# A decoder layer on one core: another order of the eight attention units, and no filler matmuls between them

## The chip, the cores and the metric

One core of a Trainium2 chip runs the whole program; nothing is shared with other cores. The metric is the device time of one execution in microseconds. A core has engines with a queue of their own each: TensorE (PE: matmuls and transposes), VectorE (DVE), ScalarE (ACT), GpSimd (POOL), and SyncE (SP), which issues the loads and stores. An engine works through its queue in order; a step that waits for a semaphore holds up all that stands behind it.

## The reference

The layer works on x of 8 batches x 128 tokens x 256 features, in three stages, each added to its input and normalized:

```python
x = layernorm(x + attn(x, Wq, Wk, Wv, Wo))      # 16 heads of 128, 4 K/V groups, rotary, softmax
x = layernorm(x + xattn(ctx, ctx, x, ssm, D))   # per head of 8 features: y_ij = conv(k_i * v_j) + D k_i v_j
                                                # out_j = sum_i y_ij * q_i     (16 heads, length 256)
x = layernorm(x + ffn(x, W_gate, W_qkv))        # top-1 gated shared key/value, causal softmax, 16 heads
```

The second stage's convolution acts on the product of context features only, and doesn't depend on x; only the last sum (its "products") does.

## The kernel before, in words

**Phase A, attention.** The work is cut into 8 units. A unit is one K/V group (4 query heads, `HG`) for one half of the batches (4 batches, `BH`). They run in the order u = 2v + j, group v = 0..3 outside, half j = 0, 1 inside, so half 0 has all its groups after unit 6, half 1 after unit 7. Within a unit k = 0..3 is the batch. For each batch there are `scores` (TensorE), `row_max` (VectorE), `exps` (ScalarE), `invert` (VectorE), `normalize` (GpSimd), `turn` (TensorE transposes the probabilities), `prob_high` (ScalarE) and `prob_low` (VectorE), which split them into a high and a low part, `values` (three matmuls; the third takes the low part), `head_copy` (ScalarE), `head_low` (VectorE), `output` (12 matmuls with Wo into an accumulation bank); `accumulate` (VectorE) adds two batches' output to x.

**Between these steps** a unit does the projections for the next unit, its "items" K, Q0 to Q3 and V. For K and Q: `project` (6 matmuls) into one of two banks that take turns, `rotate` on ScalarE (two copies into `rot`), `cos_item` on VectorE (frees the bank), `sin_item` on GpSimd (L1574) and `add_item` on VectorE (L1126). So item i + 2 waits for the cos step of item i. `rot` and `t_cos`, `t_sin` have two buffers each. Each group's weights are loaded once (`w_raw`) and split into `w_hi` (ScalarE, L835) and `w_lo` (VectorE, L1138) in even units; Wo's are split by ScalarE (`wo_hi`) and GpSimd (`wo_lo`, L1599).

**Convolutions.** The items C0 to C3 of each unit are four of the 32 convolutions (L394) of the second stage, of one matmul call (even) or two (odd). GpSimd prepares the products of context features for four of them with `pairs` (L1564, eight instructions), in two buffers.

**Unit 7** has no next unit. Here the second stage begins for batches 0 to 3: `first_stats(0)`, GpSimd's `power` for the reciprocal root, `first_apply(b)`, `x1_turn(b)` (TensorE), `mix_query(b)` (ScalarE), the products (`pair_products`, L318 and L321, 15 instructions a batch, mostly on GpSimd; the nearest three distances of batch 0 on VectorE), `mix_sum(b)` (VectorE, L1376), `mix_turn(b)`, `add_mix(b)`, statistics, `second_power`, `second_apply(b)`, `x2_turn(b)`. These turns all use one bank, `mix_bank`. Where TensorE would wait, `keep_busy(n)` (L417) puts n filler matmuls: 26 in unit 7 and behind it.

**Phase B.** `seq(i)` for i = 0..6 runs the third stage of batch i, with parts of the next batches' second and third stage between: `gate_project`, `kv_project`, `query_project`, `key_turn`, `fscores`, `fexps`, `fturn`, `fvalues`, `y_turn` and the last normalization.

The order on each engine is written out by hand, and each wait is a count on a semaphore.

Of the kernel before, what the change touches and what calls it, by code (L numbers as in the profile page):

```python
# [21 lines left out]
P = 128  # L22
# [25 lines left out]

COLS = ["K", "Q0", "Q1", "Q2", "Q3", "V"]
FRONT = ["K", "Q0", "Q1", "Q2", "Q3", "V"]  # L50
BODY = ["K", "Q0", "Q1", "Q2", "Q3", "C1", "C2", "C3", "C0", "V"]
LAST = ["C1", "C2", "C3"]
# [3 lines left out]
def decoder_kernel(nc, xt_d, x_d, wqkv_d, wo_d, toep_d, dcoef_d, ctx_d, wf_d, cos_d, sin_d, ident_d,  # L56
                   anti_d, causal_d, ties_d, out_d):
    ctx = ExitStack()
    with ctx:
# [3 lines left out]
        def sem(name):  # L63
# [60 lines left out]
        prod = q_rope[:, :, :, :].rearrange("p n h t -> p n (h t)").rearrange(  # L124
            "p n (a j i) -> p n a j i", j=HD, i=HD)
# [3 lines left out]
        qmix = rot[:, :, 0:D]  # L129
# [30 lines left out]
        first_conv_bank = acc_bank[1]  # L160
        fscore_bank = [bank[4], bank[5], bank[3]]
# [62 lines left out]
        ln3 = [sem(f"ln3_{n}") for n in ("sum", "stats", "aggr", "eps", "rstd", "out")]  # L224
        x1T_done = sem("x1T_done")
# [100 lines left out]
        def _(sp):  # L326
            def load_toep(u, j):

                if not (isinstance(u, int) and u <= 1):
                    sp.wait_ge(proj_done, proj_count(u - 2, BODY.index("C3")))  # L330
                sp.dma_start(toep[:, j, :, :], toep_d[:, bass.ds(2 * u, 2), :]).then_inc(in_toep[j], 16)
# [9 lines left out]
            load_toep(0, 0)  # L341
# [24 lines left out]
        def _(pe):  # L366
# [32 lines left out]
            def scores(u, j, k):  # L399
# [20 lines left out]
            pe.wait_ge(filler_set, 1)  # L420
            keep_busy(13)
            pe.wait_ge(x_hi_done, 1)
            pe.wait_ge(w_hi_first, 1)
            for name in COLS:
                if name == "V":
                    pe.wait_ge(cos_done, 1)
                if name == "Q2":
                    pe.wait_ge(w_lo_done, 2)
                project(0, name, front_bank[name], first=(name == "K"))
            def front_scores(k, heads):  # L430

                for h in heads:
                    if k == 0:
# [1319 lines left out]
```

## Time and profile before

| | us |
|---|---|
| median of 3 runs | 339.44 |
| lowest and highest run | 336.38, 342.62 |
| profiled execution: span from the first to the last instruction | 334.2 |
| between that span and the lowest, median, highest run | 2.2, 5.2, 8.4 |
| TensorE busy in the span | 316.0 |
| VectorE, ScalarE, GpSimd busy in the span | 253.1, 232.3, 198.7 |

The profiled execution's time outside of its span isn't recorded, so the span stands for it. Busy times of TensorE are modelled: a row's duration reaches some 0.2 us beyond the start of the next matmul's, so that its steps are best read from start to start. In the span, unit 0 starts at 21.25 us, unit 1 at 49.83, unit 2 at 75.60, unit 3 at 101.36, unit 6 at 178.64 and unit 7 at 204.38; the first `fscores` is at 233.04 and that of the second batch at 246.54.

### The profile page before, as it was taken

The page shows a single profiled execution, that of the slowest core. Times are in us where ns is not written, and L with a number is a line of the kernel's source. Part 1 is how long each engine was busy: PE and PEld are TensorE (multiplying, and loading weights), DVE is VectorE, ACT ScalarE, POOL GpSimd, SP SyncE. Part 2 cuts the span into 40 slices and gives each one's busy share as a digit, 9 for nine tenths or more (in the row PEclk, how much of TensorE's full clock was granted, in tenths as well). Part 3 has the DMA queues.
Part 4 walks back from the last instruction along what each step waited for, and adds up shares of the span by engine and source line. Part 5 has one row for each costly group of instructions (what it writes and reads, how often), then busy time and mean ns, then how long its engine had stood idle before and what let it go on. Part 6 is the DMA issues. An engine that isn't in the chain of part 4 may idle for free.

```text
span 334.2 us, 6299 instructions
## 1 busy us (share of the span) xinstructions
PE 316.0 (95%) x2099; PEld 245.1 (73%) x2099; DVE 253.1 (76%) x505; ACT 232.3 (69%) x691; POOL 198.7 (59%) x284
## 2 busy tenths in 40 slices
PE   6998999999999999999999999999699999999982
PEld 2786798898898888888889888755366566666641
DVE  2698867857867856876865776989877899998646
ACT  3679578768868957968867865531458777878781
POOL 0679835837844857754665763799790866812102
PEclk9999999999999999999999999999979999999998
DMA  6941010042010031010040000000000000000010
GB/s 178 352 194 63 2 33 0 1 127 66 0 31 0 3 127 64 0 33 0 0 138 4 1 0 2 1 2 1 0 1 2 2 16 3 17 19 18 1 33 31
DMA packets 5616, 13.08 MB, mean 39 GB/s; under 512 B 848, under 2 KB 3024, under 8 KB 5328
## 3 DMA queue, kind: packets, MB, share of 16 engines
q1 hardware_dynamic: 5312, 12.29, 11.0%
q10 hardware_dynamic: 272, 0.39, 0.4%
q8 instruction: 17, 0.28, 0.3%
q14 instruction: 15, 0.12, 0.1%
HBM read 11.63 MB, written 1.05 MB: 38 GB/s over the span
## 4 chain that ended last, share of the span: by engine, by line
PE 77%; DVE 8%; POOL 6%; issue 3%; ACT 2%; DMA 2%; POOLq 0%; DVEq 0%
PE bank L377 19%; PE bank L532 11%; PE bank L408 8%; PE bank L394 6%; PE bank L704 4%; PE bank L693 4%; PE bank L497 4%; PE bank L659 3%; POOL q_rope L318 3%; PE bank L519 3%; PE bank L714 2%; POOL q_rope L321 2%; PE bank L514 2%; PE bank L516 2%; PE bank L688 2%
## 5 line engine op out<-in xcount | busy, mean ns | idle before, releaser
L1605 POOL TENSOR_TENSOR prob<-prob,rden 128x512 f32<-128x512 f32 x32 | 34.1, 1066 | 46.3 <-DVE rden L1196 46.3
L1574 POOL TENSOR_TENSOR t_sin<-rot,sin 128x512 f32<-128x512 f32 x36 | 46.5, 1298 | 22.4 <-ACT rot L855 21.8
L888 ACT ACTIVATE prob<-bank,neg_max 128x128 f32<-128x128 f32 x128 | 45.4, 373 | 0.8 <-DVE neg_max L1189 0.7
L532 PE MATMUL bank<-wo_hi,head_hi 128*128 128x256 f32 x128 | 38.4, 300 | 1.2 <-POOL wo_lo L1599 0.8
L1025 ACT ACTIVATE prob<-bank,fneg_max 128x128 f32<-128x128 f32 x128 | 36.8, 381 | 2.2 <-DVE fneg_max L1430 2.2
L532 PE MATMUL bank<-wo_hi,head_lo 128*128 128x256 f32 x128 | 36.0, 281 | 0.0
L532 PE MATMUL bank<-wo_lo,head_hi 128*128 128x256 f32 x128 | 36.0, 281 | 0.0
L932 ACT CAST head_hi<-bank 128x512 fp32r<-128x512 f32 x32 | 18.8, 588 | 23.9 <-PE bank L519 15.8
L1564 POOL TENSOR_TENSOR kv<-ctxT 128x256 f32<-128x256 f32 (+3 forms) x64 | 35.2, 579 | 0.0
L377 PE MATMUL bank<-x_hi,w_hi 128*128 128x512 f32 x96 | 31.5, 409 | 2.8 <-DVE w_hi L1155 2.0
L408 PEld LDWEIGHTS bank<-k_rope,q_rope 128*128 128x128 f32 x240 | 31.3, 191 | 2.6
L1113 DVE TENSOR_TENSOR t_cos<-bank,cos 128x512 f32<-128x512 f32 x36 | 24.7, 687 | 11.1 <-ACT rot L855 10.5
L318 POOL TENSOR_TENSOR q_rope<-y,rot 128x64 f32<-128x64 f32 (+7 forms) x61 | 31.8, 527 | 2.0 <-ACT rot L988 2.0
L1667 POOL TENSOR_TENSOR rstd<-var_eps,half_pow 128x1 f32<-128x1 f32 (+1 forms) x18 | 10.9, 607 | 36.1 <-DVE var_eps L1361 33.1
L408 PE MATMUL bank<-k_rope,q_rope 128*128 128x128 f32 x240 | 31.6, 274 | 0.0
L1249 DVE TENSOR_TENSOR head_lo<-bank,head_hi 128x512 fp32r<-128x512 f32 x32 | 22.1, 690 | 11.7 <-ACT head_hi L932 11.2
L854 ACT COPY rot<-bank 64x512 f32<-64x512 f32 x40 | 23.4, 585 | 10.6 <-PE bank L377 8.7
L377 PE MATMUL bank<-x_lo,w_hi 128*128 128x512 f32 x96 | 30.0, 394 | 0.3 <-DVE x_lo L1138 0.3
L377 PE MATMUL bank<-x_hi,w_lo 128*128 128x512 f32 x96 | 30.0, 394 | 0.1
L1189 DVE TENSOR_REDUCE neg_max<-bank 128x4 f32<-128x512 f32 x32 | 22.0, 687 | 9.8 <-PE bank L408 9.5
L394 PE MATMUL bank<-kv,toep 128*128 128x288 f32 x96 | 27.2, 405 | 0.0
L1126 DVE TENSOR_TENSOR q_rope<-t_cos,t_sin 128x512 f32<-128x512 f32 x28 | 23.2, 850 | 5.1 <-POOL t_sin L1574 5.1
(132 smaller groups left out, 814.6 us busy)
## 6 DMA issues: line engine op xcount, KB each, us to landing
w_raw<-in_wqkv SPq DMA_DIRECT2D x3, 768.0 KB, 5.9
toep<-in_toep SPq DMA_DIRECT2D x8, 256.0 KB, 3.1
wo_raw<-in_wo SPq DMA_DIRECT2D x4, 512.0 KB, 3.5
x_raw<-in_xt SPq DMA_DIRECT2D x2, 512.0 KB, 5.5
ctxT<-in_ctx SPq DMA_DIRECT2D x1, 1024.0 KB, 4.8
x<-in_x SPq DMA_DIRECT2D x1, 1024.0 KB, 8.9
out<-x SPq DMA_DIRECT2D x8, 128.0 KB, 1.7
wf<-in_wf SPq DMA_DIRECT2D x1, 784.0 KB, 4.5
```

The lines of the kernel that those rows point to most:

```text
L318: last = eng.tensor_tensor(pr[:, :, d * HD:d * HD + (n - 1) * (HD + 1) + 1:HD + 1], y[:, :, at:at + n], q[:, :, 0:n], ALU.mult)
L377: last = pe.matmul(out[:, :], wp[:, c, col:col + P], xp[:, j, c, :], start=(c + n == 0), stop=(c == C - 1 and n == 2))
L394: last = pe.matmul(out, toep[:, j, hh, tap:tap + P], kv[:, j, m, hh * NB:(hh + 1) * NB, :], start=(m == 0), stop=(m == lb))
L408: last = pe.matmul(score_bank[k % 2][:, h * P:(h + 1) * P], q_rope[:, j, h, k * P:(k + 1) * P], k_rope[:, j, k * P:(k + 1) * P], start=Tru ...
L532: last = pe.matmul(acc_bank[k // 2][:, (k % 2) * D:(k % 2 + 1) * D], hp[:, k % 2, h * P:(h + 1) * P], wp[:, v % 2, h, :], start=(h + n == ...
L854: act.copy(rot[0:H2, par, :], bank_in[H2:P, :])
L888: last = act.activation(prob[:, k % 2, h * P:(h + 1) * P], score_bank[k % 2][:, h * P:(h + 1) * P], ACT.Exp, bias=neg_max[:, k % 2, h:h + ...
L1025: last = act.activation(prob[:, c % 2, h * P:(h + 1) * P], scored[:, h * P:(h + 1) * P], ACT.Exp, bias=fneg_max[:, c, h:h + 1])
L1113: dve.tensor_tensor(t_cos[:, par, :].rearrange("p (b t) -> p b t", b=BH), bank_in[:, :].rearrange("p (b t) -> p b t", b=BH), cos[:, :].uns ...
L1564: last = pool.tensor_tensor(kv[:, buf, :, :, at:at + n], src[:, :, :, 0:n], src[:, :, :, d:HD], ALU.mult)
L1574: pool.tensor_tensor(t_sin[:, par, :].rearrange("p (b t) -> p b t", b=BH), rot[:, par, :].rearrange("p (b t) -> p b t", b=BH), sin[:, :].u ...
L1605: pool.tensor_tensor(own, own, rden[:, k % 2, :].unsqueeze(2).to_broadcast([P, HG, P]), ALU.mult).then_inc(norm_done, 1)
```

## The change

The loops over units are written out step by step, and the order changes in these places.

- **Units.** Group and half of the eight units are now (0,0), (0,1), (1,0), (1,1), (2,0), (3,0), (3,1), (2,1). Half 0 is complete after unit 5 (`HALF_ENDS`). Group 2's weights are loaded and split a second time, in unit 5 (`W_LOADS`).
- **Convolutions.** `CONVS_OF`: unit 0 keeps five, units 1 to 3 have five each, units 4 and 5 six each, units 6 and 7 none. So `pairs` move forward on GpSimd.
- **Second stage.** `first_stats(0)`, four `first_apply`, two `x1_turn`, two `mix_query`, batch 0's products (all on GpSimd now), `mix_sum(0)` and `mix_turn(0)` move into unit 6. `qmix` gets its own buffer, and `prod`'s first buffer lies in `kv`.
- **No fillers** but for the 13 at the start. In phase B `x1_turn(4)` stands behind `mix_turn(2)` and waits, by the bank's order `MIX_ORDER`, for `add_mix(2)`. Phase B is otherwise as before from batch 1 on.

The core of the diff:

```diff
+MIX_ORDER = [("mix", 0), ("x2", 0), ("x1", 2), ("mix", 1), ("x2", 1), ("x1", 3), ("mix", 2), ("x1", 4),
+             ("x2", 2), ("x1", 5), ("mix", 3), ("x2", 3), ("x1", 6), ("mix", 4), ("x2", 4), ("x1", 7),
...
+GROUP_OF = [0, 0, 1, 1, 2, 3, 3, 2]
+HALF_OF = [0, 1, 0, 1, 0, 0, 1, 1]
+HALF_ENDS = [5, 7]
+W_LOADS = [0, 1, 2, 3, 2]
+W_SPLIT_IN = {0: 1, 2: 2, 3: 3, 5: 4}
...
+CONVS_OF = [range(1, 5), range(5, 10), range(10, 15), range(15, 20), range(20, 26), range(26, 32),
+            range(32, 32)]
...
+            def mix_bank_free(kind, b):
+
+                at = MIX_ORDER.index((kind, b))
+                if at == 0:
+                    pe.wait_ge(cos_done, len(ROPED) * UNITS)
+                    return
+                before, of = MIX_ORDER[at - 1]
+                if before == "x1":
+                    pe.wait_ge(qmix_done, of + 1)
+                elif before == "mix":
+                    pe.wait_ge(ln2[0], of + 1)
                 else:
...
+                    pe.wait_ge(x2copy_done, of + 1)
```

GpSimd's new order, units 2 and 5 to 7 (before: sin Q2, sin Q3, pairs 0 to 2, normalize(u,3), pairs 3 to 7 in each unit; `HD` is 8):

```diff
+            normalize(2, 0)
+            split_wo(1)
+            normalize(2, 1)
+            sin_item(2, "K")
+            sin_item(2, "Q0")
+            sin_item(2, "Q1")
+            normalize(2, 2)
+            pairs(3, range(0, 3))
+            sin_item(2, "Q2")
+            sin_item(2, "Q3")
+            pairs(3, range(3, HD))
+            pairs(4, range(0, 3))
+            normalize(2, 3)
+            pairs(4, range(3, HD))
...
+            split_wo(3)
+            normalize(5, 1)
+            pairs(7)
+            sin_item(5, "K")
+            sin_item(5, "Q0")
+            sin_item(5, "Q1")
+            normalize(5, 2)
...
+            sin_item(6, "K")
+            sin_item(6, "Q0")
+            first_power(0)
+            sin_item(6, "Q1")
+            normalize(6, 2)
+            sin_item(6, "Q2")
+            sin_item(6, "Q3")
+            products(0, range(0, 3))
+            normalize(6, 3)
+            products(0, range(3, HD))
+            normalize(7, 0)
+            normalize(7, 1)
             second_power(0)
...
+            products(1, range(0, 3))
+            normalize(7, 2)
+            products(1, range(3, HD))
+            normalize(7, 3)
```

Units 1 and 4 have pairs 0 to 2 ahead of sin Q2 as unit 2 has, and one `pairs` each; unit 3 is as before. TensorE's new order, unit 6 to the first batch of phase B:

```diff
+            output(6, 0)
+            turn(6, 1)
+            x1_turn(0)
+            item(6, "Q3")
+            x1_turn(1)
+            scores(6, 3)
+            values(6, 1)
+            turn(6, 2)
+            output(6, 1)
+            values(6, 2)
+            scores(7, 0)
+            turn(6, 3)
+            output(6, 2)
+            values(6, 3)
+            item(6, "V")
+            scores(7, 1)
+            v_turn(7)
+            mix_turn(0)
+            output(6, 3)
+            turn(7, 0)
+            scores(7, 2)
+            values(7, 0)
+            turn(7, 1)
+            scores(7, 3)
+            output(7, 0)
+            values(7, 1)
+            x2_turn(0)
+            turn(7, 2)
+            output(7, 1)
+            gate_project(0)
+            values(7, 2)
+            x1_turn(2)
+            turn(7, 3)
+            kv_project(0, 0)
+            kv_project(0, 1)
+            output(7, 2)
+            query_project(0)
+            mix_turn(1)
+            values(7, 3)
             key_turn(0)
...
+            x2_turn(1)
+            output(7, 3)
+            fscores(0, 0)
+            gate_project(1)
+            kv_project(1, 0)
+            x1_turn(3)
+            fscores(0, 1)
+            fturn(0, 0)
+            kv_project(1, 1)
+            query_project(1)
+            mix_turn(2)
+            x1_turn(4)
+            fturn(0, 1)
+            key_turn(1)
+            fvalues(0, 0)
+            fscores(1, 0)
```

VectorE's new order where it differs most, in units 6 and 7:

```diff
+            cos_item(6, "K")
+            prob_low(6, 0)
+            row_max(6, 2)
+            first_stats(0)
+            cos_item(6, "Q0")
+            head_low(6, 0)
...
+            prob_low(6, 2)
+            accumulate(6, 0)
+            head_low(6, 2)
+            first_apply(2)
+            first_apply(3)
+            set_mask()
+            row_max(7, 0)
+            prob_low(6, 3)
+            invert(7, 0)
+            head_low(6, 3)
+            mix_sum(0)
+            row_max(7, 1)
...
+            prob_copy(7, 2)
+            mix_sum(1)
+            accumulate(7, 0)
+            head_low(7, 2)
```

## Rows read from the trace of the kernel before

**Rows 1.** The page, busy time, share of the span and instructions of each engine.

```profile
PE 316.0 (95%) x2099; PEld 245.1 (73%) x2099; DVE 253.1 (76%) x505; ACT 232.3 (69%) x691; POOL 198.7 (59%) x284
```

**Rows 2.** Windows: bounds, length, busy time (count) of each engine, clock, DMA share, GB/s.

```profile
21.30:49.80 28.50, 27.04 (x162) 22.84 (x163) 22.88 (x35) 21.39 (x62) 21.69 (x24) 1.00 0.10 29
75.60:101.30 25.70, 25.70 (x162) 22.44 (x161) 18.82 (x33) 20.25 (x59) 17.08 (x18) 1.00 0.10 32
204.40:233.00 28.60, 27.32 (x158) 18.64 (x156) 26.47 (x57) 10.93 (x40) 23.92 (x47) 1.00 0.00 1
244.00:246.00 2.00, 2.00 (x10) 1.67 (x9) 1.85 (x7) 0.58 (x2) 2.00 (x5) 0.50 0.00 0
```

**Rows 3.** Timeline of GpSimd in unit 2: start, duration, line, idle before.

```profile
75.98 2.40 POOL L1599 TENSOR_TENSOR wo_lo<-wo_raw,wo_hi 128x1024 fp32r<-128x1024 f32 x1 [3.61 <-ACT wo_hi L841]
...
79.33 2.54 POOL L1574 TENSOR_TENSOR t_sin<-rot,sin 128x512 f32<-128x512 f32 x2
...
86.52 2.65 POOL L1574 TENSOR_TENSOR t_sin<-rot,sin 128x512 f32<-128x512 f32 x2
89.12 2.49 POOL L1564 TENSOR_TENSOR kv<-ctxT 128x256 f32<-128x256 f32 x3
91.58 1.04 POOL L1605 TENSOR_TENSOR prob<-prob,rden 128x512 f32<-128x512 f32 x1
92.58 1.89 POOL L1564 TENSOR_TENSOR kv<-ctxT 128x160 f32<-128x160 f32 x5
```

**Rows 4.** Timeline of VectorE in unit 2.

```profile
81.86 0.68 DVE L1126 TENSOR_TENSOR k_rope<-t_cos,t_sin 128x512 f32<-128x512 f32 x1
...
89.46 1.79 DVE L1126 TENSOR_TENSOR q_rope<-t_cos,t_sin 128x512 f32<-128x512 f32 x2
...
91.26 0.65 DVE L1242 TENSOR_TENSOR probT_lo<-bank,probT_hi 128x512 fp32r<-128x512 f32 x1
```

**Rows 5.** Timeline of TensorE in unit 2: Q3, convolutions, third values matmul, turn.

```profile
84.96 0.71 PE L377 MATMUL bank<-x_hi,w_hi 128*128 128x512 f32 x2
...
88.03 1.62 PE L394 MATMUL bank<-kv,toep 128*128 128x288 f32 x6
89.49 0.60 PE L497 MATMUL bank<-ident,prob 128*128 128x128 f32 x4
...
91.97 0.50 PE L519 MATMUL bank<-probT_lo,v_hi 128*128 128x512 f32 x1
...
94.17 0.60 PE L497 MATMUL bank<-ident,prob 128*128 128x128 f32 x4
```

**Rows 6.** Timelines of GpSimd, VectorE and TensorE in unit 0.

```profile
28.15 2.38 POOL L1599 TENSOR_TENSOR wo_lo<-wo_raw,wo_hi 128x1024 fp32r<-128x1024 f32 x1
...
29.05 2.03 DVE L1126 TENSOR_TENSOR k_rope<-t_cos,t_sin 128x512 f32<-128x512 f32 x1
...
33.18 0.73 PE L377 MATMUL bank<-x_hi,w_hi 128*128 128x512 f32 x2 [0.48 <-DVE t_cos L1113]
```

**Rows 7.** Timeline of ScalarE at the end of unit 2, a weight split.

```profile
100.62 0.84 ACT L835 CAST w_hi<-w_raw 128x768 fp32r<-128x768 f32 x1
```

**Rows 8.** Timeline of VectorE in unit 7.

```profile
205.30 1.41 DVE L1332 BATCH_NORM_STATS2 stats<-x 128x6 f32<-128x256 f32 x4
206.74 0.38 DVE L1336 BATCH_NORM_AGGREGATE mean_var<-stats 128x2 f32<-128x6 f32 x4
...
217.88 2.29 DVE L1376 TENSOR_REDUCE t_cos<-q_rope 128x256 f32<-128x2048 f32 x1
```

**Rows 9.** Groups by line: fillers of 204 to 234, products of 225.4 to 232.3.

```profile
L417 PE MATMUL bank<-filler 128*128 128x512 bf16 x26 | 6.6, 379 | 0.0
...
L318 POOL TENSOR_TENSOR q_rope<-y,rot 128x256 f32<-128x256 f32 (+7 forms) x8 | 4.2, 538 | 0.0
L321 POOL TENSOR_TENSOR q_rope<-y,rot 128x32 f32<-128x32 f32 (+6 forms) x8 | 3.9, 481 | 0.0
```

**Rows 10.** Waits of TensorE, 204 to 262: total, times, longest.

```profile
PE bank L624 <- DVE x L1345: 2.3, 1, 2.3
PE bank L642 <- DVE x L1366: 1.0, 2, 0.8
PE bank L650 <- ACT k_rope L992: 0.5, 1, 0.5
```

More of the change, by code:

```diff
@@ new lines, in _ @@
+            output(7, 3)
[13 more added lines that the diff above has]
+            fscores(1, 0)
+            x2_turn(2)
+            fturn(0, 2)
+            fvalues(0, 1)
+            gate_project(2)
@@ new lines, in _ @@
+            x1_turn(5)
+            kv_project(2, 0)
+            fturn(0, 3)
+            fvalues(0, 2)
+            fscores(1, 1)
+            fturn(1, 0)
+            kv_project(2, 1)
+            query_project(2)
+            fvalues(0, 3)
+            mix_turn(3)
+            fturn(1, 1)
+            key_turn(2)
+            fvalues(1, 0)
+            y_turn(0)
+            fscores(2, 0)
+            x2_turn(3)
+            fturn(1, 2)
+            fvalues(1, 1)
+            gate_project(3)
@@ new lines, in _ @@
+            x1_turn(6)
+            kv_project(3, 0)
+            fturn(1, 3)
+            fvalues(1, 2)
+            fscores(2, 1)
+            fturn(2, 0)
+            kv_project(3, 1)
+            query_project(3)
+            fvalues(1, 3)
+            mix_turn(4)
+            fturn(2, 1)
+            key_turn(3)
+            fvalues(2, 0)
+            y_turn(1)
+            fscores(3, 0)
+            x2_turn(4)
+            fturn(2, 2)
+            fvalues(2, 1)
+            gate_project(4)
@@ new lines, in _ @@
+            x1_turn(7)
+            kv_project(4, 0)
+            fturn(2, 3)
+            fvalues(2, 2)
+            fscores(3, 1)
+            fturn(3, 0)
+            kv_project(4, 1)
+            query_project(4)
+            fvalues(2, 3)
+            mix_turn(5)
+            fturn(3, 1)
+            key_turn(4)
+            fvalues(3, 0)
+            y_turn(2)
+            fscores(4, 0)
+            x2_turn(5)
+            fturn(3, 2)
+            fvalues(3, 1)
+            gate_project(5)
@@ new lines, in _ @@
+            second_apply(1)
+            accumulate(7, 1)
+            frow_max(0, 0)
+            frow_max(0, 1)
+            first_stats(1)
+            gating(1)
+            mix_sum(2)
+            first_apply(4)
+            frow_max(0, 2)
+            share(1)
+            add_mix(2)
+            mix_norm(2)
+            frow_max(0, 3)
+            first_apply(5)
+            second_apply(2)
+            frow_max(1, 0)
+            frow_max(1, 1)
+            mix_sum(3)
+            gating(2)
@@ new lines, in _ @@
+            frow_max(1, 2)
+            share(2)
+            add_mix(3)
+            mix_norm(3)
+            frow_max(1, 3)
+            first_apply(6)
+            y_invert(0)
+            y_scale(0)
+            second_apply(3)
+            frow_max(2, 0)
+            frow_max(2, 1)
+            mix_sum(4)
+            gating(3)
+            frow_max(2, 2)
+            ffn_norm(0)
+            share(3)
+            add_mix(4)
+            mix_norm(4)
+            frow_max(2, 3)
+            first_apply(7)
```

1947 lines of the change are left out of this document (1266 added, 681 removed).

## The prediction

> **What bounds the kernel now.** I read the page first, then the windows by stage, then the timelines of single engines. The page [rows 1] has TensorE busy for 95% of the span. By stage [rows 2]: unit 2, which stands for units 1 to 6, is 25.7 us long and TensorE is busy in all of it, while VectorE has 18.8 and GpSimd 17.1. So in units 1 to 6 nothing but TensorE's own work counts, as long as each result arrives before TensorE comes to it. Unit 0 has 28.5 us instead of 25.7: the same work, one convolution more (0.5 us, below), and a GpSimd that is busy for 21.7. That is the row to remember: where GpSimd falls behind, TensorE loses. Unit 7 and the start of the second phase are the weak place: 28.6 us from 204.4 to 233, of which 26 matmuls are fillers [rows 9], and behind it are waits of 2.3 and 1.0 us [rows 10] and a stretch at half clock [rows 2].
>
> What is there to win? In the PE timeline of unit 7 the filler groups stand in gaps of 1.6, 1.7, 0.7, 1.5, 1.3 and 0.7 us, 7.7 with a short wait (26 fillers at some 0.24 us are 6.2, the rest is waiting around them). Behind 233 there are 0.5, 2.3, 0.8 and 0.2 us of waiting [rows 10], 0.2 us once more, and about 2 us that the half clock costs. In all some 13 us. From then on the two orders are the same, and so is the end.
>
> **Part 1: the convolutions move, at no cost in sum.** A convolution is one or two matmul calls, by turns, and three calls take from 88.03 to 89.49 [rows 5], 0.49 us each. `CONVS_OF` gives units 1 to 5 in turn 2, 1, 2, 3 and 3 calls more than before, 11 in all or 5.35 us; units 6 and 7 lose 6 and 5. It is not free in its place: in unit 6 the convolutions were work for TensorE while ScalarE did the exponentials (Part 6).
>
> **Part 2: GpSimd's order in units 1, 2 and 4.** Before, GpSimd does sin Q2 and Q3 and then `pairs` (86.52 and 89.12) [rows 3]. Now the first three instructions of `pairs`, 2.49 us, stand ahead of sin Q2. The normalization before them is tied to ScalarE and ends at 86.5, so sin Q3 ends at 86.5 + 2.5 + 2.6 = 91.65, not 89.17. On VectorE `add_item(Q3)` waits for it and stands in front of `invert` and `prob_low(u,2)`. The two adds began at 89.46 and `prob_low` at 91.26 [rows 4]; now the second add begins at 91.7 and `prob_low` at 92.65, ending at 93.3. TensorE's third matmul of `values(u,2)` came at 91.97, right behind it [rows 5]. It loses 93.37 - 91.97 = 1.4 us, in each of the three units: **4.2 us**.
>
> **Part 3: unit 2 has two `pairs`.** Between `normalize(2,2)` and `normalize(2,3)` GpSimd now has 2.49 + 2.6 + 1.9 + 2.49 = 9.5 us: it ends the latter at 97.1. The turn that needs it came at 94.17 [rows 5], and with 1.4 us of stall and one call less ahead of it comes at 95.1. It waits **2.0 us** more. The second half of pairs(4) ends before the next normalization is due.
>
> **Part 4: unit 5.** After `split_wo` and `normalize(5,1)`, which end at 79.37 in unit 2's times [rows 3], all eight instructions of pairs(7) (2.49 + 1.89 = 4.4 us) come ahead of sin K. It ends at 85.04 instead of 80.6, sin Q0 at 86.3. On VectorE add K and add Q0 wait for them and cos Q1 stands behind: it ends at 87.6, and only then is the bank free for the projection of Q3, which began at 84.96 [rows 5]. 2.7 us. ScalarE's rotation of Q1 waits for sin K too, so exponentials, Q2 and Q3 come late and cost 0.15 and 0.45 more: **3.3 us**. The nearest row is unit 0, where half of `pairs` and the `wo` split stand around sin K and the same projection waits (at 33.18) [rows 6]; that unit lost 28.5 - 25.7 - 0.5 = 2.3.
>
> **Part 5: weights of group 2 a second time.** A load of 768 KB and two splits on ScalarE and VectorE more. Unit 2 has such splits and no wait on TensorE [rows 2], so nothing; but at the end of unit 3 the `wo` split and the second half of the `w` split now both precede `exps(4,1)`, one copy of 0.84 us [rows 7]. Bounds 0 and 0.84; the rotation of K and prob_high(4,0) had 0.1 to 0.4 us to spare, so 0.45. Units 1 to 5 together: 4.2 + 2.0 + 3.3 + 0.45 = **10 us**.
>
> **Part 6: units 6 and 7 without fillers.** I walked both units with durations from the rows, queue by queue, from unit 6's first matmul (178.64). Unit 6: `first_stats(0)` (1.4 and 0.5 us) [rows 8] now stands before cos Q0, and the projection of Q2 waits 1.4; x1_turn(0) waits 0.3; without convolutions behind scores(6,3), output(6,1) waits 1.2 for head_low; exps(6,3), normalize(6,3) and head_low(6,2) cost 0.8 together; three steps of VectorE (two applies, the mask) before prob_low(6,3) cost 0.5; mix_turn(0) waits 1.5 for mix_sum(0), which takes 2.3 [rows 8]. All eight distances of batch 0's products are on GpSimd now, 8.1 us busy a batch but 6.9 from first to last start [rows 9], and the normalizations of unit 7 stand between them. Unit 7: values(7,0) 0.5, output(7,0) 1.1, turn(7,2) 1.0 and turn(7,3) 1.7, both behind products(1), kv_project(0) 1.4 (accumulate(7,0) stands behind mix_sum(1)), x2_turn(1) 1.7. That gives fscores(0,0) at 231.2 instead of 233.0. Then mix_turn(2) waits 2.0, as mix_sum(2) stands behind the four statistics and gating(1); x1_turn(4), which stood ahead of the second batch's projection, now waits for add_mix(2) (the bank's order), and that stands behind first_apply(4), a row maximum and share(1): 3.9 us; key_turn(1) waits 1.5 for ScalarE. fscores(1,0) comes at 246.65; before it came at 246.54. Its clock stretch I leave as it is, since a wait of this kind is in both. Behind it the waits of 0.8, 0.2 and 0.2 us go: **-1.1**. So out of 13 us in reach, little is got: the waits are small and many instead of few and filled, and the 5.35 us of convolutions that left these units are used up.
>
> **The sum.** 5.35 (calls moved forward) + 10.0 + 0.1 - 1.1 = +14.3 us on the profiled execution: 334.2 to 348.5 of span. The lowest run shown is 2.2 us above the span and the median 5.2 us; the difference is added to the median: 339.4 + 14.3 = **353.7 us**, 4% slower.
>
> One more thing bears on these terms. In unit 0 an add of two SBUF operands on VectorE took 2.03 us while GpSimd ran the 2.38 us split; alone it took 0.68 [rows 4, 6]. "SBUF — State Buffer" in the Trainium skill, section "SBUF: two separate sides", calls the pair that VectorE and GpSimd share an exclusive lock, held for a whole instruction, when VectorE reads two SBUF inputs. The trace agrees. By that rule adds K, Q2 and Q3 in units 1, 2, 4 and 5 would each wait for one instruction of GpSimd more, up to 1.3 us; the estimate by it would be some 3 us higher, 356.7 us, which lies inside my forecast's own band and so is no rival of its own.
>
> **The rivals.**
> (a) The waits in units 1 to 5 come as said, but the walk of units 6 and 7 is too pessimistic, since each of its some fifteen waits is a chain of estimates. If half of the 20 us of waits in it don't happen: 353.7 - 10 = 344, within 2%. For it: in before, TensorE lost 13 us here in all, and 20 is more. Against: VectorE is busy for 26.5 of unit 7's 28.6 us [rows 2], so in any order something stands behind it.
> (b) Faster. GpSimd's moves are hidden, because `pairs` waits for nothing and GpSimd has 8.6 us idle in a unit [rows 2], and the early half does what the gaps want: all of 13 us gained, nothing lost: 339.4 - 13 = 326. It decides at the wait behind add Q3: if sin Q3 ended 1.4 us earlier than I have it, no unit would lose. Against: the normalization ahead is bound by ScalarE's exponentials, so GpSimd can't run ahead; and unit 0 shows the loss.
> (c) The clock. Before, after 2.3 us of waiting [rows 10], TensorE fell to 0.50 of its clock, 1.2 GHz, from about 242 to 246 [rows 2]; with the fillers it kept 2.4 GHz through unit 7. Without them the waits of 1 to 2 us in units 6 and 7 and the 3.9 us one could bring two or three such stretches, each costing what this one cost, some 2 us, plus what is late behind it: 353.7 + 6 = 360. Against: in unit 0 waits of 0.5 to 0.8 us close together left it at 1.00. "TensorE: Matmul & The Clock Gate" in the Trainium skill, on a second failure mode, says that brief idling between matmul groups can be enough to make the clock swing; no row here shows that for gaps under 2.3 us.
> (d) The losses in units 1 to 5 are real but half of mine, because GpSimd's steps run closer together or a later step absorbs them: 353.7 - 5 = 348.7. And should the early half not be early at all, since unit 6 begins 15 us later: its first_stats then still comes before unit 7, and the walk holds.
>
> **How the numbers follow.** Forecast 0.5 (350 to 358). (a) 0.17, (b) 0.07, (c) 0.13, (d) 0.13. Two percent, about what a measurement here can tell from no change, is 332.6 to 346.2. Faster is (b): 0.07. Within: most of (a), a little of (d) and of mixtures: 0.2. Slower: 0.73. For 8 in 10 the range leaves out (b), the lower part of (a) and the end of (c): 343 to 361; the bound of the weights (0 to 0.84 us) and of the lock (0 to 3) lie in it.
>
> **What the profile would show.** Units 1, 2, 4 and 5 longer than their work by 1.4, 3.4, 1.9 and 3.3 us, unit 3 by none; in them waits of the third values matmul for probT_lo, of the turn in unit 2 for `prob` from GpSimd, of a projection in unit 5 for t_cos. A start of unit 6 at 178.6 + 15.3 = 194. After unit 7, a wait of x1_turn(4) for add_mix(2) of more than 3 us, and a clock below 1 behind it. From the second batch on, 11.2 us a batch and no waits. It would be wrong if units 1 to 5 show no TensorE waits (then (b)), or if fscores(0,0) comes much earlier than 52.6 us after unit 6's start.

## The result, and the profile after

| | before | after |
|---|---|---|
| median of 4 runs, us | 338.64 | 360.81 |
| lowest and highest, us | 336.38, 342.62 | 359.28, 361.10 |
| profiled span, us | 334.2 | 359.0 |

The ratio is 1.068, 95% interval 1.063 to 1.073: some 22 us slower, against 14.3 in the forecast. (The ratio leaves out the slow run of 342.62 us; by the other three, median 337.85, it is 23 us.) The direction was right, the size was not: 360.8 lies above the 350 to 358 that the forecast gave. The page of the changed kernel, busy time and the row of clocks in 40 slices of 9 us:

```profile
PE 324.6 (90%) x2073; PEld 247.2 (69%) x2073; DVE 258.7 (72%) x502; ACT 234.0 (65%) x693; POOL 201.0 (56%) x289
PEclk9899999999999999999899999999955999999998
```

TensorE lost five points of busy share against [rows 1], and two slices of the clock row show 5, which is half of it; an 8 or a 9 is a slice with a shorter stretch at half clock, or none. The starts of units and of `fscores`, read from the timeline of TensorE in both kernels, divide the 24.8 us of span:

| stretch | before | after | difference | forecast |
|---|---|---|---|---|
| start of unit 1 | 49.83 | 50.95 | +1.1 | 0 |
| units 1 to 5 in all (27.51, 28.53, 27.07, 29.52, 31.25 long) | 128.8 | 143.9 | +15.1 | +15.35 |
| of this, 11 convolution calls | | | +5.35 | +5.35 |
| of this, the rest | | | +9.7 | +10.0 |
| start of unit 6 to `fscores(1, 0)` | 67.9 | 72.1 | +4.2 | +0.1 |
| from there to the start of the third batch's `fscores` | 12.2 | 16.5 | +4.3 | -1.1 |
| from there to the end | | | +0.1 | 0 |

The first row is no effect of the change: unit 1 starts between 49.6 and 51.2 us in every kernel of this study, at 50.9 or later in the three profiles (this one, runs 1 and 6) that have a stretch of 3.4 us at half clock between 8 and 13 us, and before 49.9 in the others. It is clock all the same. Units 1 to 5 are the forecast's. The row of unit 6 to `fscores(1, 0)` and the row behind it are 8.5 us against -1.0, and that is most of the miss. The windows over this place (columns as in [rows 2]):

```profile
236.00:240.00 4.00, 1.85 (x9) 0.84 (x8) 2.61 (x2) 0.95 (x3) 4.00 (x9) 1.00 0.00 0
240.00:244.00 4.00, 3.67 (x6) 1.62 (x7) 2.85 (x6) 0.87 (x3) 2.45 (x5) 0.57 0.01 2
...
256.00:260.00 4.00, 2.96 (x18) 1.94 (x16) 3.48 (x7) 0.99 (x3) 4.00 (x8) 1.00 0.00 0
260.00:264.00 4.00, 0.79 (x4) 0.82 (x5) 3.85 (x12) 0.09 (x1) 2.65 (x8) 0.63 0.00 0
264.00:268.00 4.00, 2.98 (x18) 1.06 (x16) 2.09 (x3) 3.35 (x13) 3.99 (x7) 0.50 0.00 0
268.00:272.00 4.00, 4.00 (x23) 2.46 (x23) 2.00 (x3) 1.25 (x5) 3.53 (x10) 0.50 0.01 2
272.00:276.00 4.00, 4.00 (x18) 2.53 (x15) 2.29 (x5) 1.56 (x7) 0.00 (x0) 0.50 0.02 4
276.00:280.00 4.00, 4.00 (x25) 2.08 (x25) 0.69 (x1) 2.36 (x8) 0.00 (x0) 0.74 0.00 0
```

Read the clock, the third number from the right. It also gives the length of a stretch at half clock: 0.57 over 4 us is 2 x 4 x 0.43 = 3.4 us at 0.50 (1.2 GHz). Before, apart from the end of the span, it was low only for 3.4 us, from about 243 to 246. Now it is low for 3.4 us within 240 to 244, and again from about 261 to 278, for 17 us, although TensorE is busy for all of 268 to 278. A stretch of 3.4 us lies in unit 5 too, behind a wait of 1.83 us that is shown below:

```profile
176.00:180.00 4.00, 4.00 (x17) 3.45 (x15) 3.76 (x8) 1.85 (x4) 3.55 (x3) 0.61 0.00 0
```

To return to the long one. Its columns are work that takes longer, and VectorE, ScalarE and GpSimd have little to do beside it. The timeline of TensorE shows what came ahead (the brackets are idle time and what ended it):

```profile
259.52 0.44 PE L587 MATMUL bank<-ident,t_cos 128*128 128x128 f32 x2 [1.00 <-DVE t_cos L1781]
263.21 0.66 PE L577 MATMUL bank<-ident,x 128*128 128x128 f32 x2 [3.25 <-DVE x L1787]
263.66 1.06 PE L671 MATMUL bank<-ident,prob 128*128 128x128 f32 x4
265.75 0.66 PE L636 MATMUL bank<-ident,krep 128*128 128x128 f32 x2 [1.02 <-ACT w_raw L1219]
```

These are `mix_turn(2)`, `x1_turn(4)` and `key_turn(1)`, the three waits that the walk has last, 5.3 us in a stretch of some 7. The waits of TensorE from unit 6 to here, grouped (total, times, longest), answer to [rows 10]:

```profile
PE bank L577 <- DVE x L1787: 3.2, 1, 3.2
PE bank L510 <- POOL prob L2316: 2.6, 3, 1.2
PE bank L587 <- DVE t_cos L1781: 2.1, 2, 1.1
PE bank L549 <- DVE head_lo L1723: 1.6, 2, 1.0
PE bank L402 <- DVE t_cos L1595: 1.6, 1, 1.6
PE bank L596 <- DVE x L1768: 1.5, 1, 1.5
PE bank L618 <- DVE x L1697: 1.3, 1, 1.3
PE bank L636 <- ACT w_raw L1219: 1.0, 1, 1.0
```

Each has its place in Part 6.

In the units before, the waits are the predicted ones in kind, not in share. Unit 5, in the timelines of TensorE, VectorE and GpSimd:

```profile
175.00 0.72 PE L402 MATMUL bank<-x_hi,w_hi 128*128 128x512 f32 x2 [1.83 <-DVE t_cos L1595]
...
172.06 1.69 DVE L1608 TENSOR_TENSOR k_rope<-t_cos,t_sin 128x512 f32<-128x512 f32 x1 [2.17 <-POOL t_sin L2288]
173.67 0.68 DVE L1608 TENSOR_TENSOR q_rope<-t_cos,t_sin 128x512 f32<-128x512 f32 x1
174.27 0.68 DVE L1595 TENSOR_TENSOR t_cos<-bank,cos 128x512 f32<-128x512 f32 x1
...
167.33 3.39 POOL L2278 TENSOR_TENSOR kv<-ctxT 128x256 f32<-128x256 f32 x8
170.68 2.52 POOL L2288 TENSOR_TENSOR t_sin<-rot,sin 128x512 f32<-128x512 f32 x2
```

It is the chain of Part 4 link by link: `pairs(7)`, sin K, add K, add Q0, cos Q1, the projection of Q3. And unit 2, GpSimd and TensorE:

```profile
89.40 1.64 POOL L2278 TENSOR_TENSOR kv<-ctxT 128x256 f32<-128x256 f32 x3
91.00 2.50 POOL L2288 TENSOR_TENSOR t_sin<-rot,sin 128x512 f32<-128x512 f32 x2
93.46 4.30 POOL L2278 TENSOR_TENSOR kv<-ctxT 128x160 f32<-128x160 f32 x8
97.71 1.04 POOL L2316 TENSOR_TENSOR prob<-prob,rden 128x512 f32<-128x512 f32 x1
...
98.81 0.66 PE L510 MATMUL bank<-ident,prob 128*128 128x128 f32 x4 [0.89 <-POOL prob L2316]
```

The first three instructions of `pairs`, which took 2.49 us in [rows 3], took 1.64 in their new place. So sin Q3 ends 15.0 us behind the unit's start (13.6 before, 16.05 in the forecast) and `prob_low` begins at 16.5 (15.7 before, 17.05 in the forecast). TensorE, with one convolution call more ahead of it, doesn't wait for it here.

### The profile page after: what moved, and what is told of

It is laid out like the page before. It is cut to its first block, busy times and chain, and to the rows that moved or that the text cites. A ratio compares the mean times of both kernels' runs of the same rounds, so it can differ in the third digit from the quotient of the medians.

```text
span 359.0 us, 6269 instructions
## 1 busy us (share of the span) xinstructions
PE 324.6 (90%) x2073; PEld 247.2 (69%) x2073; DVE 258.7 (72%) x502; ACT 234.0 (65%) x693; POOL 201.0 (56%) x289
## 4 chain that ended last, share of the span: by engine, by line
PE 55%; DVE 16%; POOL 12%; issue 11%; ACT 5%; DMA 2%; POOLq 0%; DVEq 0%; ACTq 0%
PE bank L402 12%; PE bank L549 6%; PE bank L439 5%; POOL t_sin L2288 4%; PE bank L424 4%; PE bank L660 4%; PE bank L618 4%; PE bank L671 4%; POOL kv L2278 3%; PE bank L683 2%; PE bank L655 2%; DVE q_rope L1608 2%; POOL q_rope L329 2%; DMA w_raw<-in_wqkv 2%; PE bank L533 2%
## 5 line engine op out<-in xcount | busy, mean ns | idle before, releaser
L2288 POOL TENSOR_TENSOR t_sin<-rot,sin 128x512 f32<-128x512 f32 x36 | 47.3, 1324 | 21.4 <-ACT rot L1129 19.6
L2278 POOL TENSOR_TENSOR kv<-ctxT 128x256 f32<-128x256 f32 (+3 forms) x64 | 33.2, 551 | 0.3 <-PE bank L424 0.3
L439 PE MATMUL bank<-k_rope,q_rope 128*128 128x128 f32 x240 | 32.5, 279 | 0.0
L402 PE MATMUL bank<-x_lo,w_hi 128*128 128x512 f32 x96 | 31.1, 406 | 0.3 <-DVE x_lo L1621 0.3
L1838 DVE TENSOR_REDUCE fneg_max<-bank 128x4 f32<-128x512 f32 x32 | 21.1, 682 | 14.2 <-PE bank L660 14.2
L402 PE MATMUL bank<-x_hi,w_lo 128*128 128x512 f32 x96 | 30.8, 402 | 0.0
L1608 DVE TENSOR_TENSOR q_rope<-t_cos,t_sin 128x512 f32<-128x512 f32 x28 | 24.5, 894 | 4.8 <-POOL t_sin L2288 4.8
```

The lines of the kernel that those rows point to most:

```text
L402: last = pe.matmul(out[:, :], wp[:, c, col:col + P], xp[:, j, c, :], start=(c + n == 0), stop=(c == C - 1 and n == 2))
L439: last = pe.matmul(score_bank[k % 2][:, h * P:(h + 1) * P], q_rope[:, j, h, k * P:(k + 1) * P], k_rope[:, j, k * P:(k + 1) * P], start=Tru ...
L1608: dve.tensor_tensor(dst, t_cos[:, par, :], t_sin[:, par, :], ALU.add).then_inc(rope_done, 1)
L2278: last = pool.tensor_tensor(kv[:, buf, :, :, at:at + wide], src[:, :, :, 0:wide], src[:, :, :, d:HD], ALU.mult)
L2288: pool.tensor_tensor(t_sin[:, par, :].rearrange("p (b t) -> p b t", b=BH), rot[:, par, :].rearrange("p (b t) -> p b t", b=BH), sin[:, :].u ...
```

## The experiments

My theory after this comparison: three causes. Some 10 us are waits in units 1 to 5, made by GpSimd's order; 5.35 us are calls moved; some 8 us are the clock, not in the sum at all. Each run was timed against the kernel before on the same chip. No kernel leaves computation out; fillers are matmuls of no use into a free bank (`keep_busy_y` writes the accumulation bank once the last output has been read). Medians in us:

| run | median | ratio to before, 95% interval | profiled span, clock |
|---|---|---|---|
| changed kernel | 360.81 | 1.068 (1.063 to 1.073) | 359.0, 0.959 |
| 1 before, without fillers | 337.81 | 1.002 (0.998 to 1.007) | 338.9, 0.976 |
| 2 GpSimd's order in units 1, 2, 4 | 358.12 | 1.062 (1.053 to 1.070) | 354.2, 0.975 |
| 3 `pairs(7)` earlier | 356.30 | 1.056 (1.050 to 1.062) | 354.5, 0.968 |
| 4 one gap filled | 356.79 | 1.059 (1.049 to 1.069) | 354.5, 0.980 |
| 5 six gaps filled | 352.31 | 1.044 (1.038 to 1.050) | 350.3, 0.993 |
| 6 waits of units 1 to 5 out | 353.04 | 1.046 (1.039 to 1.053) | 353.3, 0.968 |
| 7 both of these | 346.51 | 1.026 (1.020 to 1.031) | 344.7, 0.993 |
| 8 `x1_turn(4)` in its old place | 353.88 | 1.048 (1.041 to 1.056) | 352.2, 0.980 |
| 9 run 7 with `x1_turn(4)` so | 345.33 | 1.024 (1.020 to 1.029) | 343.7, 0.997 |
| 10 run 7, `normalize` earlier | 351.03 | 1.041 (1.036 to 1.047) | 349.9, 0.987 |
| 11 run 7, edits of 9 and 10 | 349.07 | 1.036 (1.029 to 1.043) | 347.3, 0.992 |
| 12 three gaps around the long wait filled | 353.55 | 1.050 (1.045 to 1.055) | 351.9, 0.985 |

**Run 1.** The kernel before with its six `keep_busy` calls behind the start taken out:

```diff
-keep_busy(5)
...
-keep_busy(6)
...
-keep_busy(2)
...
-keep_busy(5)
...
-keep_busy(6)
...
-keep_busy(2)
```

> The kernel before, with its 26 fillers in unit 7 and behind it taken out, and nothing else (the 13 at the start stay). Theory 1, the half clock comes from one long wait of TensorE and not from the fillers' absence: unit 7's gaps (1.7 us at most) leave the clock at 1.00, the stretch at half clock behind the 2.3 us wait stays as long as it was (4.3 us), time 338 to 340, ratio 0.995 to 1.005. Theory 2, the fillers kept the clock up: a stretch at half clock appears in unit 7 or the one behind 241 us grows to 10 us or more, and the time is 342 to 346, ratio 1.01 to 1.02.

No difference in time. The profiled execution was the slowest of ten, and it is neither theory's: from the end of unit 6 to 237 us the clock is at 1.00, though TensorE waits four times for 1.3 to 1.6 us there, and then it is low twice, for 3.4 and 6.8 us, where the kernel before had 3.4 once. The second time follows a wait of 1.49 us:

```profile
250.45 0.44 PE L637 MATMUL bank<-ident,x 128*128 128x128 f32 x2 [1.49 <-DVE x L1360]
```

The windows behind it:

```profile
252.00:256.00 4.00, 4.00 (x16) 2.56 (x12) 2.58 (x5) 1.65 (x7) 0.00 (x0) 0.50 0.02 4
256.00:260.00 4.00, 4.00 (x25) 1.97 (x25) 0.69 (x1) 2.46 (x9) 0.00 (x0) 0.77 0.00 0
```

So leaving the fillers out of the kernel before costs nothing that these runs can tell, and a gap need not reach 2.3 us to bring the clock down.

**Run 2.** GpSimd's order in units 1, 2 and 4 nearly as before; unit 1 shown:

```diff
-pairs(2, range(0, 3))
 sin_item(1, "Q2")
 sin_item(1, "Q3")
-pairs(2, range(3, HD))
+pairs(2, range(0, 3))
 normalize(1, 3)
+pairs(2, range(3, HD))
```

> The changed kernel, with GpSimd's order of before in units 1, 2 and 4: sin Q2 and Q3 ahead of pairs, and pairs(4) whole behind pairs(3) after normalize(2,3). Theory 1: units 1, 2 and 4 lose 0.8, 2.3 and about 1.5 us of waits, 4 to 5 us in sum, and the end comes that much earlier, 356 to 357, ratio to the kernel before 1.053. Rival: the later units wait on other engines and give it back, less than 1.5 us is gained.

Units 1 and 4 became 0.34 and 0.31 us shorter, not 1.4; unit 2 became 0.25 longer. There TensorE waits at the second convolution of that unit:

```profile
96.16 0.72 PE L424 MATMUL bank<-kv,toep 128*128 128x288 f32 x2 [1.86 <-issue]
```

The trace names no releaser; the convolution is the first to use what `pairs(3)` prepares, and with the order of this run that is ready later. Part 2 had looked only at what waits behind `pairs`, not at who waits for it. The median is 2.7 us lower than the changed kernel's with intervals that overlap, so the units' lengths in the profile are the result here, not the median.

This run shows one thing more, of the clock. TensorE waits 1.19 and 1.27 us ahead of `turn(7, 3)` and `kv_project(0, 0)` as in the changed kernel, and yet the stretch at 240 isn't there, and the projection takes 1.98 us instead of 3.59:

```profile
238.44 1.98 PE L618 MATMUL bank<-wf,k_rope 128*128 128x512 f32 x4 [1.27 <-DVE x L1697]
```

The window:

```profile
236.00:240.00 4.00, 2.22 (x9) 1.26 (x9) 3.96 (x5) 1.18 (x5) 4.00 (x7) 1.00 0.00 0
```

The same waits, then, can pass without a low stretch. The four runs of this one kernel go with it: 356.04, 357.17, 359.07 and 360.64 us at mean clocks of 0.975, 0.973, 0.963 and 0.958.

**Run 3.** One line moved:

```diff
+pairs(7)
 split_wo(3)
 normalize(5, 1)
-pairs(7)
```

> The changed kernel, with one step of GpSimd moved: pairs(7) goes ahead of split_wo(3) and normalize(5,1), into GpSimd's idle time at the end of unit 4, from behind them. Theory 1: unit 5 goes from 31.25 us to 27.2 to 28, as the projection of Q3 no longer waits, 3.3 to 4 us in all, 357, ratio 1.056. Rival: the wo split is late by about 1 us and with it sin K, and half of it stays.

Unit 5 is 27.95 us long instead of 31.25: 3.3 us, the number of Part 4. Some 0.3 of it is the stretch at half clock in the changed kernel's unit 5: in runs 2 and 4, whose profiles have the same order there and no such stretch, the unit is 30.91 us long. Add K on VectorE, which took 1.69 us above, took 0.68 here, with next to no work of GpSimd beside it:

```profile
168.62 0.68 DVE L1608 TENSOR_TENSOR k_rope<-t_cos,t_sin 128x512 f32<-128x512 f32 x1
```

**Runs 4, 5 and 12: the clock.** Only fillers are added to the changed kernel; the other engines' orders stay. Run 4 has those of the longest wait, run 12 also those on its two sides, run 5 also those before `turn(7, 3)`, `kv_project(0, 0)` and `x2_turn(1)`:

```diff
+keep_busy_y(4)     # runs 5 and 12
 mix_turn(2)
+keep_busy_y(14)    # runs 4, 5 and 12
 x1_turn(4)
 fturn(0, 1)
+keep_busy_y(5)     # runs 5 and 12
 key_turn(1)
```

> The changed kernel with 14 fillers (3.0 us) in one place, ahead of x1_turn(4), where TensorE waits 3.25 us; they write a bank that is free there. Theory 1, that one wait lowers the clock for the 16 us behind it: the clock is 1.00 from 262 to 278, the second and third batches of the last stage come 4 to 5 us earlier and the time is 356, ratio 1.053. Rival, the clock falls for the many short waits together, since TensorE is idle for a quarter of the time from unit 6 on: a stretch at half clock of 8 us or more stays somewhere, gain under 2 us.

> The changed kernel with fillers in six places where TensorE waits from the end of unit 7 on: turn(7,3), kv_project(0), x2_turn(1), mix_turn(2), x1_turn(4), key_turn(1), 39 in all (8.3 us) in gaps of 9.3 us. Theory 1 (clock): the granted clock is 1.00 from 236 to 280, the kv projection takes 1.9 instead of 3.6 us, the second batch's fscores comes 2 us earlier and the third batch's 4 to 5 us more: 353 to 354, ratio 1.047. Rival (the waits are what costs, and the clock only fills them): less than 3 us is gained, ratio above 1.055.

> The changed kernel with fillers only around its longest wait: 4 before mix_turn(2), 14 before x1_turn(4), 5 before key_turn(1). Theory: the clock stayed at half for 16 us because two waits of about 1 us stood beside the one of 3.25 us, so with all three filled the stretch from 260 goes and the one at 240 stays: 354 to 356 us, less than the 356.79 of the run that filled the longest alone. Rival: the clock falls at the next unfilled wait instead (those of 1.0 to 1.5 us at 249 or at 240), and stays low for as long: 357 to 361 us.

In run 4 the gap of 3.25 us is full of matmuls, and the clock falls all the same, behind the next wait, but for 6.8 us instead of 17. The timeline has that wait, the windows the clock:

```profile
263.60 0.41 PE L643 MATMUL bank<-ident,krep 128*128 128x128 f32 x2 [1.44 <-ACT w_raw L1227]
```

```profile
264.00:268.00 4.00, 3.89 (x25) 2.19 (x24) 1.50 (x4) 2.28 (x7) 4.00 (x9) 0.69 0.00 0
268.00:272.00 4.00, 4.00 (x19) 2.40 (x19) 2.98 (x5) 2.09 (x7) 1.63 (x6) 0.50 0.03 6
272.00:276.00 4.00, 4.00 (x30) 2.35 (x29) 0.69 (x1) 2.73 (x10) 0.00 (x0) 0.96 0.00 0
```

In run 12, with all three filled, there is no low stretch here; behind unit 7 only that of 239 to 242 is left:

```profile
240.00:244.00 4.00, 4.00 (x17) 2.50 (x16) 2.91 (x6) 0.67 (x3) 1.26 (x3) 0.71 0.01 2
...
264.00:268.00 4.00, 3.74 (x36) 2.16 (x36) 2.03 (x5) 2.94 (x10) 4.00 (x8) 1.00 0.02 4
268.00:272.00 4.00, 4.00 (x31) 2.30 (x31) 2.97 (x7) 3.43 (x14) 2.21 (x7) 1.00 0.01 2
```

And in run 5 the clock stays at 1.00 throughout this part. Its units 1 to 5 are as in the changed kernel (27.5, 28.5, 27.1, 29.5, 31.1 us), but unit 6 to `fscores(1, 0)` takes 69.9 us instead of 72.1, and from there to the third batch 11.4 instead of 16.5. By the medians of the runs it is 8.5 us, by the ratios 8.3: that is what the clock cost in the changed kernel, by a step that changed nothing else but fillers. In the profiled pair it is 8.7 us of span: 7.3 in the two rows of the miss, and 1.3 ahead of unit 1, where no filler was added. Of the whole, 6 to 7 (ratio 1.068 to 1.050, median 360.81 to 353.55; 5.9 us in the profiles, over the two rows) is the long stretch around `x1_turn(4)`.

**Runs 6 and 7: do the causes add?** Run 6 takes the waits of units 1 to 5 out: `pairs(7)` as in run 3, units 1 and 4 as in run 2, in unit 2 the whole of `pairs(4)` behind `normalize(2, 3)`, and in unit 4 the second split of the weights later, on ScalarE (shown) and on VectorE:

```diff
-split_w(3, 1)
 exps(4, 1)
+split_w(3, 1)
```

Run 7 has the fillers of run 5 too.

> The changed kernel without fillers, with the waits of units 1 to 5 taken out as far as the order allows: pairs(7) early, sin Q2 and Q3 ahead of pairs in units 1 and 4, pairs(4) whole behind normalize(2,3), and the second weight split of unit 3 behind exps(4,1) on ScalarE and behind invert(4,1) on VectorE. Theory 1: units 1 to 5 lose 9.7 us now; pairs(7) gives 3.3, the split 1.0, normalize(2,3) 0.9, the rest under 0.5 each: 6 us in sum, 354, ratio 1.05. Rival: units 6 and 7 take it back, ratio above 1.06.

> Both: the order of e6 and the fillers of e5. If the two causes are independent their gains add: 359 - 6 - 6 = 347 to 349, ratio 1.03. What then is left over the kernel before, some 10 us, is the rest of units 1 to 5 (4 us) and the waits of units 6 and 7. If the clock's stretches come from the whole of the waits, the gains add to less.

The five units are now 27.18, 27.44, 27.14, 28.52 and 27.96 us in run 7, 138.2 in sum instead of 143.9. Run 6 gained 7.8 us, more than the 6 of its theory (5.7 between the profiled spans); the stretches at half clock in and behind unit 7 are still in its profile, for 3.4 and 13.7 us. The medians fall by 7.8, 8.5 and, with both, 14.3 us: they nearly add. The runs with the clock held also agree closely with each other: run 7's four lie within 0.2 us (346.40 to 346.59), run 9's within 0.3, while run 2's lie between 356.04 and 360.64. Its clock row, beside the one above:

```profile
PEclk9999999999999999999999999999999999999997
```

**Runs 8 and 9: `x1_turn(4)` in its old place**, ahead of the second batch's projection:

```diff
-MIX_ORDER = [... ("mix", 2), ("x1", 4), ...
+MIX_ORDER = [... ("x1", 4), ("mix", 2), ...
 fturn(0, 0)
+x1_turn(4)
 kv_project(1, 1)
 query_project(1)
 mix_turn(2)
-x1_turn(4)
```

> The changed kernel with one part undone: x1_turn(4) stands behind fturn(0,0) as before, ahead of the second batch's projection, and MIX_ORDER accordingly. Theory 1: add_mix(2) is no longer waited for, TensorE waits there for first_apply(4) instead, which comes at about the same time behind first_power(1), since GpSimd has to do four distances of batch 3's products first; the second batch's kv_project and so share(1) come later. Gain between -2 and +2 us, 359 to 362. Rival: the place of x1_turn(4) is the cause of the long wait and of the clock, gain 5 us or more.

The wait doesn't go, it changes its releaser and grows, from 3.25 to 3.70 us:

```profile
259.29 0.56 PE L577 MATMUL bank<-ident,x 128*128 128x128 f32 x2 [3.70 <-DVE x L1744]
```

Its windows:

```profile
256.00:260.00 4.00, 0.71 (x3) 0.70 (x4) 3.43 (x4) 0.32 (x2) 4.00 (x9) 0.93 0.00 0
260.00:264.00 4.00, 4.00 (x18) 2.74 (x16) 2.20 (x6) 1.89 (x7) 1.46 (x5) 0.64 0.00 0
264.00:268.00 4.00, 3.23 (x34) 1.75 (x32) 3.92 (x10) 2.55 (x8) 3.22 (x6) 1.00 0.01 2
```

And yet the time falls by 6.9 us: behind the wait there is now work instead of two more waits, and the clock is back at 1.00 from 263 on, after 3.4 us instead of 17. Was it the order or the clock? Run 9 asks that, with the clock held in both:

> The kernel of the seventh experiment (waits of units 1 to 5 out, gaps of unit 6 filled; 346.51 us) with x1_turn(4) put ahead of kv_project(1, 1) again, as in the kernel before the change; 14 fillers stand in front of it and those around it are left out. Theory: with no stretch at half clock left, this order is worth only what the longer wait costs, so 345 to 346.5 us, first_apply(4) late by about 3.7 us whichever call waits. Rival: the order itself is worth the 7 us that the eighth experiment gained, so about 340 us.

Only 1.2 us by the medians, 0.4 by the ratios. So of the 6.9 some 6 are the clock.

**Runs 10 and 11: is the rest GpSimd's queue in unit 7?**

```diff
-products(1, range(0, 3))
 normalize(7, 2)
-products(1, range(3, HD))
+products(1, range(0, 3))
 normalize(7, 3)
+products(1, range(3, HD))
```

> The kernel of the seventh experiment with GpSimd's queue of unit 7 changed: normalize(7, 2) ahead of products(1, 0:3) and normalize(7, 3) ahead of products(1, 3:). Theory: what is left over the time before comes from GpSimd's queue behind units 6 and 7; the waits on GpSimd's prob there (0.8 and 1.2 us) go, 344.5 to 345.5 us. Rival: mix_sum(1) then comes as much later and x1_turn(1)'s chain gives it back, 346 to 347.5 us.

> The kernel of the seventh experiment with both edits of the ninth and tenth. Theory: the two are at different places of the end of the kernel and add, 343.5 to 345.5 us, still about 2% over the kernel before. Rival: they meet in the same chain of the last batches (the later of the two alone counts), then no lower than the better of the two.

Both theories missed: run 10 is 4.5 us slower than run 7, and lies above its rival's range as well. `turn(7, 2)` and `turn(7, 3)` did come without waits, but `mix_sum(1)` starts late (at 232.84 us instead of 230.40), `accumulate(7, 0)` stands behind it, and `kv_project(0, 0)` waits for that, in a gap that has no fillers (timeline, then windows):

```profile
235.78 2.93 PE L625 MATMUL bank<-wf,k_rope 128*128 128x512 f32 x3 [2.87 <-DVE x L1711]
```

```profile
232.00:236.00 4.00, 1.13 (x6) 0.42 (x4) 3.16 (x3) 0.00 (x0) 4.00 (x9) 0.88 0.00 0
236.00:240.00 4.00, 4.00 (x8) 1.93 (x9) 1.63 (x6) 0.87 (x3) 0.90 (x2) 0.50 0.03 6
240.00:244.00 4.00, 4.00 (x24) 3.47 (x24) 2.06 (x6) 0.39 (x1) 0.00 (x0) 0.77 0.00 0
```

The rival had the mechanism (it is given back) but no clock in its price: one wait of 2.87 us, and 6.8 us at half clock that begin about 0.7 us before its end. I had made the forecast's own mistake once more. Run 11 is between runs 9 and 10: the same wait (2.86 us) is in it, with 3.4 us at half clock behind it, half of run 10's.

## Why the forecast came out too low

**What held.** The calls moved (5.35 us), and the sum of the waits in units 1 to 5: 9.7 us against 10.0. Unit 3 loses only 0.3 of it. Part 4 was right in its mechanism. That its number came out (run 3: 3.3 us) is in part luck: `pairs(7)` took 3.39 us instead of 4.4, add K took 1.69 instead of the 0.68 of [rows 4], the projection of Q3 began 2.1 us later in its unit than in unit 2 of before and not 2.7, and some 0.3 of the 3.3 is the clock. In Part 6 the waits of the walk came, in their places and, where it names one, with its releaser, though for the three steps that it prices at 0.8 together the trace has one wait of 0.61 for `prob` and one of 0.16: the projection of Q2 1.58 (1.4 predicted), output(6,1) 0.96 (1.2), mix_turn(0) 1.13 (1.5), turn(7,3) 1.21 (1.7), kv_project(0) 1.27 (1.4), x2_turn(1) 1.52 (1.7), x1_turn(4) 3.25 (3.9), and with larger misses output(7,0) 0.64 (1.1) and mix_turn(2) 1.00 (2.0). Rival (a), that half of them might not happen, was wrong, and so were (b) and (d). The idle times of the profile sum to 16.4 us against 20.5; each understates the lateness, since a row's duration is modelled some 0.2 us beyond the next start. That this makes up the difference is argued, not tested.

**The step that failed.** Part 6 says: "Its clock stretch I leave as it is, since a wait of this kind is in both." A wait of this kind was in both; the stretch was not the same. The term that it put at nothing measured some 8 us. Before, one wait of 2.3 us with work behind it was followed by 3.4 us of low clock. After, waits of 1.0, 3.25 and 1.0 us in a row had 17 us of it, and a second stretch of 3.4 came at 240 in front of them, behind waits of 1.21 and 1.27 us. Run 5 prices these, with what other stretches its runs had less of, at 8.5 us by the medians; in the profiles it is 7.3 us at this place. With the clock held there, the span is 350.3 against the forecast's 348.5. So with this one term the forecast would have been 362. What is left, 1.8 us of span, is the walk: in run 5 unit 6 to `fscores(1, 0)` is 2.0 us longer than before, and the walk had 0.1. Its `fscores(0, 0)` comes 54.3 us after the start of unit 6, as before (54.4), and not after 52.6.

**Rival (c)** named the cause, "two or three such stretches", and its 360 was near by the number. But its price, 2 us each from the one stretch in the trace of before, which it read as 4 us where the windows have 3.4, was wrong for the long one, which cost 6 to 7, and its "against", that gaps of 0.5 to 0.8 us close together in unit 0 leave the clock alone, said nothing about gaps of 1.0 to 3 us. Its chance of 0.13 was too small for what Part 6 has: a wait longer than the one that had halved the clock already.

**Shares that were wrong inside a sum that was right.** Part 2's 1.4 us a unit was 0.3 (run 2, units 1 and 4; in unit 2 the order couldn't be taken back without another wait). The 2.49 us of `pairs` came from a row in which VectorE adds at the same time; in the new place they took 1.64. Part 3's 2.0 us were 1.1 (unit 2 in run 7 against the changed kernel, 27.44 and 28.53, the two `pairs` in another order). In their place stand things that I hadn't counted. Unit 4 lost 2.3 us instead of 1.85: the 0.45 for the weights was a middle between 0 and 0.84, and moving that one split, with 0.3 from GpSimd's order, gave 1.0 us back. Unit 5 lost 4.0 instead of 3.3, some 0.3 of it by the clock. And all five units with fresh convolutions keep 0.4 to 1.3 us over their calls of convolutions when all that is taken out (run 7). Candidates are the step that adds the skip term, now earlier on VectorE, and single-call convolutions that leave less time for the bank behind them; a wait of 0.21 us for t_cos ahead of a convolution shows the latter in units 2 and 4. I didn't test them apart.

**The lock.** The paragraph beside the sum would have made it 356.7. Its rows are borne out (add K 1.69 us beside GpSimd's sine steps, 0.68 without them), but units 1 to 5 would then have had 13 us of waits, and they had 9.7. It counts one direction only: `pairs` ran faster (1.64 us instead of 2.49) where VectorE had no add of two SBUF operands beside it. That this makes the difference is argued, not tested.

**Where the gain went.** Even run 9, without the waits, with fillers and with `x1_turn(4)` in its old place, is 2.4% slower than before. Its unit 6 to `fscores(1, 0)` takes 68.1 us, before it took 67.9, although 5.35 us of convolutions no longer lie in it. So the second stage's early half saves nothing there. My reading, which no run tests by itself, is that work that filled TensorE's gaps was taken away, and the gaps that remain belong to chains of VectorE and GpSimd that are as long as they were. The convolutions' 5.35 us are paid in units 1 to 5, where TensorE has no gaps, and about 4 us of waits with them. Run 9's interval, 2.0 to 2.9%, begins at the 2% that these measurements can just tell. No version here beats the kernel before.

## What to carry to other kernels

Cost a wait on TensorE with its clock: look at what stands around it. Here a gap of 3.25 us with gaps of 1.0 us on both sides cost 6 to 7 us by the clock alone, and filling it moved the low stretch to the next, while one of 3.70 us followed by solid work had a stretch of 3.4 us. Take a range for it and not one number: the same waits had 3.4 us of half clock in one profile and none in another, or 3.4 and 6.8. Before moving work out of a stretch with gaps into one without, ask what the gaps are then filled with: the moved work is paid in full where it lands, and the stretch that it left may get no shorter, as here. And take a duration from a row in which the same neighbours run, since GpSimd's and VectorE's steps here differ by a third to more than double with what is beside them.

## What was not expected of the hardware

- At half clock TensorE was busy for 10 us in full (268 to 278) before the clock rose. The stretch lasted 17 us with three waits (1.0, 3.25, 1.0) around its start, 6.8 behind one of 1.44 (run 4), 3.4 behind one of 3.70 (run 8), 3.4 behind one of 2.3 [rows 2, 10], and 6.8 and 3.4 around one of 2.87 and 2.86 (runs 10 and 11). Behind waits of 1.2 to 1.3 us it came in the changed kernel and not in run 2. So the length doesn't follow the longest wait, nor the waits alone, and the rule stays open.
- The spread between runs of one kernel goes with the clock: the kernel before took 335.73 us at a mean clock of 0.989 and 339.10 at 0.981, run 2 356.04 at 0.975 and 360.64 at 0.958; with the gaps filled, run 7's four agreed within 0.2 us at 0.993 to 0.997.
- Three `pairs` instructions took 1.64 us instead of 2.49 in another place, with nothing changed in them; in the first VectorE did two adds of SBUF operands beside them [rows 3, 4], in the second none.
